# A post-norm attention and feed-forward layer on one core: the instruction lists of all five engines in a new order

## The chip, the cores and the metric

One core of a Trainium2 chip runs one launch of the kernel. The metric is the device time of that launch in microseconds; the median of 3 runs of the kernel before is 277.16 us (276.86 to 277.42). The core has TensorE (PE in the profile), VectorE (DVE), ScalarE (ACT), GpSimd (POOL) and SyncE (SP), whose queue here issues the DMA transfers of the main part.

## The reference

The input `x` is 8 x 1024 x 128 in fp32. One attention head of width 128 and a feed-forward part with a hidden width of 512, each followed by a residual sum and a layer norm, are applied to each of the 8 batches:

```python
q = fractional_rope(einsum('btd,hdk->bhtk', x, wq)) * dh ** -0.5
k = fractional_rope(einsum('btd,hdk->bhtk', x, wk)) * dh ** -0.5
v = einsum('btd,hdk->bhtk', x, wv)
s = einsum('bhik,bhjk->bhij', q, k) - 1e30 * mask      # causal: j > i is masked
o = einsum('bhij,bhjv->bihv', softmax(s), v)
x = layernorm(x + o @ wo)
bw1 = mean(|w1|, axis=1) * sign(w1); bw2 = mean(|w2|, axis=1) * sign(w2)
h = gelu(x @ bw1.T + b1, approximate=False)
x = layernorm(x + h @ bw2.T + b2)
```

The rotation turns the first half of the width only; the second half is left as it is. `wv` and `wo` are multiplied into one matrix `wvo` in the kernel's setup.

## The kernel before

Each of the 8 batches goes through the same chain of steps, and each step is a small Python function of one engine, called with a row or half number and the batch `c`. Every engine's program is a list of such calls, written out by hand in one block per engine; the engines meet through semaphores. Batches overlap: while batch c is in its feed-forward part, batch c+1 is in its scores and batch c+2 in its projections. B is 8, so `B - 1` is batch 7, `B - 4` batch 4 and so on.

The steps of one batch, in order of their data:
- SP loads `xq` (`stripes`, L222) and `xa` (`tokens`, L228). VectorE turns `xq` into `xT` with stream transposes (`x_squares`, L1579). ScalarE rounds it (`xT_high`, L1029) and GpSimd takes the rest (`xT_low`), so that fp32 products are made of three passes (high by high, low by high, high by low).
- TensorE: `project(half, c)` (L654), 12 matmuls into a pair of PSUM banks. VectorE multiplies with cosine and sine (`rotate`, L1597), GpSimd adds (`rotation_sum`), ScalarE copies what isn't rotated into `tok` (`tok_copy`, L1036).
- TensorE: `turn_qk(n, c)` (L668), four transposes into one bank. ScalarE `qkT_high` (L1052), VectorE `qkT_low` (L1617).
- TensorE: `scores(r, c)` (L578), three passes per row block r of 128 queries, up to 1024 columns. VectorE `row_max` (L1451), ScalarE `exponentials` (L994) with the row sum, VectorE `turn_row` (L1460), 32 x 32 transposes, whose blocks SP carries to `probT` by DMA (`carry`, L233). In batches 0 and 7, rows 4 to 7 are transposed by TensorE (`turn_row`) and copied by VectorE and ScalarE (`row_copy`).
- TensorE: `weigh_group(half, ...)` (L593), or `weigh_row(r, c)` (L612) where TensorE turned the rows; ScalarE `pxT_copy` (L1045); TensorE `project_out` (L625); VectorE `residual1` (L1478), `statistics1`, GpSimd `first_factors`, VectorE `first_norm` (L1494).
- TensorE `turn_x1` (L635), ScalarE `x1T_high` (L1058), VectorE `x1T_low` (L1558); TensorE `up(f, c)` (L642), ScalarE `gelu` (L1064) and `hidden_high` (L1071), GpSimd `hidden_low`; TensorE `down` (L678), ScalarE `y_half` (L1089), TensorE `turn_y` (L714), VectorE `residual2`, `statistics2`, GpSimd `second_factors`, ScalarE `second_norm` (L1096), SP `store` (L245).
- The last batch does its feed-forward part in halves: `up_half` (L694), `gelu_half` (L1077), `hidden_high_half` (L1083, on VectorE L1514), `hidden_low_half` (VectorE, L1520), `down_quarter` (L704).

PSUM holds three pairs of banks and two single banks, and TensorE takes them in turn in the order of its calls. Whoever takes a pair waits first until what was put there three pair tasks before has been read: for a projection that is `tok_copy`, for scores the `exponentials`, for `up` the `gelu` (`wait_freed`, L495):

```python
def next_pair(*task):
    pair_of[task] = pairs[len(pair_of) % len(pairs)]
    if len(pair_of) > len(pairs):
        wait_freed(*list(pair_of)[-1 - len(pairs)])
    return pair_of[task]
```

So the order of TensorE's calls sets also which reader a call waits for. `fill(n)` (L557) issues n bf16 matmuls of 512 columns on constants into a free pair; nobody reads their results. ScalarE's exponential and GELU need different tables, so each change between `exponentials` and `gelu` loads a table.

Calls of TensorE's list that the prediction speaks of, with their lines: `fill(2)` L735, `project(1, 3)` L790, `scores(6, 2)` L788, `turn_qk(3, 3)` L805, `turn_x1(1, 1)` L816, `turn_qk(3, B - 3)` L862, `turn_x1(1, B - 2)` L947, `project_out(0, B - 1)` L949, `turn_x1(0, B - 1)` L962, `project_out(1, B - 1)` L963, `up_half(0, 0, B - 1)` L964, `fill(7)` L969, `fill(2)` L972. Of ScalarE's: `xT_high(0, 1)` L1125, `tok_copy(1, 3)` L1180, `gelu(0, B - 2)` L1377, `y_half(0, B - 3)` L1378, `second_norm(0, 3)`. Of VectorE's: `rotate(1, 0)` L1629, `x_squares(0, 1)` L1630, `rotate(1, 3)` L1730.

Of the kernel before, what the change touches and what calls it, by code (L numbers as in the profile page):

```python
# [16 lines left out]
def attention_ffn_kernel(nc, x, wq, wk, wv, wo, w1, b1, w2, b2, cos_t, sin_t, out):  # L17
# [10 lines left out]
    B, T, D = x.shape  # L28
# [27 lines left out]
    with ctx:  # L56
# [147 lines left out]
        def _(sp):  # L204
# [53 lines left out]
            stripes(2)  # L258
            carry(0, 0)
            stripes(3)  # L260
            tokens(1)
# [6 lines left out]
            carry(1, 2)  # L268
            stripes(B - 2)
            tokens(3)  # L270
            carry(0, 3)
            carry(1, 3)
            stripes(B - 1)
            carry(0, B - 4)
            tokens(B - 4)
            tokens(B - 3)
            carry(1, B - 4)
            carry(0, B - 3)
            tokens(B - 2)
            store(0)  # L280
            carry(1, B - 3)
            carry(0, B - 2)
            store(1)
            carry(1, B - 2)
            store(2)
            tokens(B - 1)
            carry(0, B - 1)
# [10 lines left out]
        def _(pool):  # L298
# [99 lines left out]
            xT_low(0, 2)  # L398
            xT_low(1, 2)
            rotation_sum(0, 2)  # L400
            xT_low(0, 3)
            xT_low(1, 3)
            first_factors(0, 0)
            rotation_sum(1, 2)
            rotation_sum(0, 3)
            first_factors(1, 0)
            xT_low(0, B - 4)
            xT_low(1, B - 4)
            rotation_sum(1, 3)
            first_factors(0, 1)  # L410
            first_factors(1, 1)
            rotation_sum(0, B - 4)
            rotation_sum(1, B - 4)
# [3 lines left out]
            xT_low(0, B - 3)  # L417
            hidden_low(3, 0)
            first_factors(0, 2)
            xT_low(1, B - 3)  # L420
            first_factors(1, 2)
            rotation_sum(0, B - 3)
            xT_low(0, B - 2)
# [6 lines left out]
            rotation_sum(1, B - 3)  # L430
            first_factors(1, 3)
            xT_low(1, B - 2)
            hidden_low(0, 2)
            rotation_sum(0, B - 2)
# [4 lines left out]
            xT_low(0, B - 1)  # L439
            first_factors(0, B - 4)  # L440
            second_factors(1)
            first_factors(1, B - 4)
            xT_low(1, B - 1)
            rotation_sum(0, B - 1)
# [4 lines left out]
            second_factors(2)  # L449
            first_factors(0, B - 3)  # L450
            rotation_sum(1, B - 1)
# [33 lines left out]
        def _(pe):  # L485
# [257 lines left out]
            setup_turn_sgn1()  # L743
# [6 lines left out]
            turn_row(4, 0)  # L750
            turn_row(5, 0)
            turn_qk(1, 1)
# [7 lines left out]
            scores(2, 1)  # L760
            weigh_group(0, 0, 3, 0)
            scores(3, 1)
            scores(4, 1)
            scores(5, 1)
            project_out(0, 0)
            scores(6, 1)
            turn_qk(0, 2)
            scores(7, 1)
            weigh_row(4, 0)
            project(1, 2)  # L770
            weigh_row(5, 0)
            weigh_row(6, 0)
            weigh_row(7, 0)
            turn_qk(1, 2)
# [15 lines left out]
            project(1, 3)  # L790
            weigh_group(1, 0, 3, 1)
            turn_x1(1, 0)
            weigh_group(1, 4, 7, 1)
            up(0, 0)
            up(1, 0)
            project_out(1, 1)
            turn_qk(0, 3)
            up(2, 0)
            project(0, B - 4)
            turn_qk(1, 3)  # L800
            turn_qk(2, 3)
            up(3, 0)
            scores(0, 3)
            scores(1, 3)
            turn_qk(3, 3)  # L805
            weigh_group(0, 0, 3, 2)
            scores(2, 3)
            turn_x1(0, 1)
# [5 lines left out]
            scores(6, 3)  # L814
            weigh_group(1, 0, 3, 2)
            turn_x1(1, 1)  # L816
# [5 lines left out]
            up(1, 1)  # L822
            project_out(1, 2)
            turn_qk(2, B - 4)
            project(0, B - 3)
            up(2, 1)
            down(0, 0)
            scores(0, B - 4)
            down(1, 0)
            scores(1, B - 4)  # L830
            up(3, 1)
# [3 lines left out]
            turn_y(1, 0)  # L835
            weigh_group(0, 0, 3, 3)
# [4 lines left out]
            weigh_group(1, 0, 3, 3)  # L841
            scores(5, B - 4)
            scores(6, B - 4)
            weigh_group(1, 4, 7, 3)
# [16 lines left out]
            scores(0, B - 3)  # L861
            turn_qk(3, B - 3)  # L862
            scores(1, B - 3)
# [10 lines left out]
            weigh_group(1, 0, 3, B - 4)  # L874
            project(1, B - 2)
            weigh_group(1, 4, 7, B - 4)
            turn_qk(0, B - 2)
            up(0, 3)
            turn_qk(1, B - 2)
            up(1, 3)  # L880
            project_out(1, B - 4)
            up(2, 3)
            down(0, 2)
            up(3, 3)
            turn_qk(2, B - 2)
            turn_qk(3, B - 2)
            project(0, B - 1)
            down(1, 2)
            turn_y(0, 2)
            scores(0, B - 2)  # L890
            scores(1, B - 2)
            scores(2, B - 2)
            turn_y(1, 2)
            weigh_group(0, 0, 3, B - 3)
            scores(3, B - 2)
            turn_x1(0, B - 4)
            scores(4, B - 2)
# [5 lines left out]
            weigh_group(1, 0, 3, B - 3)  # L903
            turn_qk(0, B - 1)
            weigh_group(1, 4, 7, B - 3)
            up(0, B - 4)
            up(1, B - 4)
            turn_qk(1, B - 1)
            project(1, B - 1)
# [4 lines left out]
            up(2, B - 4)  # L914
            up(3, B - 4)
            scores(0, B - 1)
            turn_y(1, 3)
            weigh_group(0, 0, 3, B - 2)
            scores(1, B - 1)
            turn_qk(2, B - 1)  # L920
            scores(2, B - 1)
            turn_qk(3, B - 1)
            scores(3, B - 1)
            project_out(0, B - 2)
            scores(4, B - 1)
            weigh_group(1, 0, 3, B - 2)
            scores(5, B - 1)
            weigh_group(1, 4, 7, B - 2)
# [1202 lines left out]
```

## Time and profile before

| | us |
|---|---|
| median of 3 runs | 277.16 (276.86 to 277.42) |
| span of the profiled execution | 274.5 |
| PE busy (matmuls) | 260.9, 95% |
| DVE busy | 229.6, 84% |
| ACT busy | 224.7, 82% |
| POOL busy | 167.2, 61% |

The span is that of one execution under the profiler; a run's time has 2.7 us more around it. Matmuls overlap in the array, so that the start of one and the start of the next tell more than the busy time: in a timeline each row gives the start in us, the duration, the engine, the line, the operation with output and inputs, the shape, the count, and in brackets the idle time before it and what ended it.

### The profile page before, as it was taken

What the parts mean: (1) busy time and instruction counts of PE and PEld (TensorE: products, weight loads), DVE (VectorE), ACT (ScalarE), POOL (GpSimd) and SP (SyncE); (2) the same over time, 40 slices, a digit from 0 to 9 for tenths busy, and PEclk for the clock granted to TensorE, in tenths of its full rate; (3) what the DMA queues carried; (4) which work ended last, traced back from release to release, by engine and by line L of the source; (5) the groups of instructions that cost most, each with busy time, mean ns of one, the idle gap of its engine ahead of it and who ended that gap; (6) DMA issues with size and microseconds to landing.
All of it is one profiled execution on the core that took longest, in us unless ns stands there. A gap on an engine that the chain in (4) does not pass through costs nothing.

```text
span 274.5 us, 5184 instructions
## 1 busy us (share of the span) xinstructions
PE 260.9 (95%) x1485; PEld 208.7 (76%) x1487; DVE 229.6 (84%) x638; ACT 224.7 (82%) x398; POOL 167.2 (61%) x258
## 2 busy tenths in 40 slices
PE   7899999999999999999999999999999999999960
PEld 3678989987779588868879688868886878897630
DVE  2799999999999996999979987998689738537984
ACT  3378964565897989996998999898999799999972
POOL 3033132613625698399821998497819887887772
PEclk9999999999999999999999999999999999999997
DMA  7944596479657936833685318825830720200323
GB/s 178 166 61 87 107 145 98 115 163 192 104 132 160 199 94 153 180 47 78 173 187 127 82 39 249 184 71 151 189 73 27 197 55 2 76 2 0 111 90 108
DMA packets 58012, 31.94 MB, mean 116 GB/s; under 512 B 33408, under 2 KB 54400, under 8 KB 57984
## 3 DMA queue, kind: packets, MB, share of 16 engines
q1 hardware_dynamic: 57024, 30.76, 50.4%
q10 hardware_dynamic: 960, 0.85, 1.3%
q8 instruction: 12, 0.20, 0.3%
q14 instruction: 16, 0.13, 0.2%
HBM read 9.18 MB, written 4.19 MB: 49 GB/s over the span
## 4 chain that ended last, share of the span: by engine, by line
PE 81%; DVE 6%; ACT 5%; issue 3%; DMA 2%; ACTq 1%; POOL 0%; POOLq 0%
PE pair L589 18%; PE bank L606 18%; PE bank L632 5%; PE bank L674 4%; PE pair L650 4%; PE pair L651 4%; PE bank L620 4%; PE bank L682 4%; PE bank L683 4%; PE bank L719 2%; DMA sin_sb<-in_sin_dram 2%; PE pair L663 2%; PE pair L665 2%; PE pair L664 2%; PE bank L639 2%
## 5 line engine op out<-in xcount | busy, mean ns | idle before, releaser
L391 POOL TENSOR_TENSOR hid_lo<-hid,hid_hi 128x1024 fp32r<-128x1024 f32 x28 | 66.0, 2386 | 19.7 <-ACT hid_hi L1075 19.7
L1004 ACT ACTIVATE prob<-pair,negmax 128x128 f32<-128x128 f32 (+3 forms) x64 | 47.2, 742 | 14.2 <-DVE negmax L1457 12.5
L606 PE MATMUL bank<-probT,xa 128*128 128x512 f32 (+3 forms) x160 | 54.2, 482 | 0.0
L1457 DVE CUSTOM_DVE_ANT_0 pair<-pair,mask_row 128x128 f32<-128x128 f32 (+3 forms) x64 | 47.9, 759 | 6.1 <-PE pair L589 5.5
L606 PEld LDWEIGHTS bank<-probT,xa 128*128 128x128 f32 x160 | 29.1, 190 | 20.2 <-issue 15.3
L341 POOL TENSOR_TENSOR xT_lo<-xT,xT_hi 128x512 fp32r<-128x512 f32 x14 | 18.0, 1288 | 40.4 <-ACT xT_hi L1034 40.4
L1467 DVE STREAM_TRANSPOSE turned<-prob 128x128 f32<-128x128 f32 (+7 forms) x56 | 39.5, 724 | 0.5 <-ACT prob L1004 0.5
L589 PE MATMUL pair<-qkT_hi 128*128 128x512 f32 (+3 forms) x96 | 36.0, 375 | 0.8 <-DVE qkT_lo L1619 0.3
L1068 ACT ACTIVATE hid<-pair,b_sb,alpha 128x1024 f32<-128x1024 f32 x28 | 32.9, 1209 | 0.1
L589 PE MATMUL pair<-qkT_lo,qkT_hi 128*128 128x512 f32 (+3 forms) x96 | 32.8, 342 | 0.0
L589 PE MATMUL pair<-qkT_hi,qkT_lo 128*128 128x512 f32 (+3 forms) x96 | 32.8, 342 | 0.0
L1075 ACT ACTIVATE hid_hi<-hid 128x1024 fp32r<-128x1024 f32 x28 | 28.6, 1057 | 0.0
L335 POOL TENSOR_TENSOR ln<-ln,minus_half 128x4 f32<-128x4 f32 (+1 forms) x21 | 26.2, 1249 | 1.6
L1102 ACT ACTIVATE res<-res,ln 128x128 f32<-128x128 f32 x52 | 23.1, 496 | 3.6 <-POOL ln L377 3.6
L1056 ACT ACTIVATE qkT_hi<-bank 128x512 fp32r<-128x512 f32 x32 | 18.5, 598 | 7.3 <-PE bank L674 7.2
L1619 DVE TENSOR_TENSOR qkT_lo<-bank,qkT_hi 128x512 fp32r<-128x512 f32 x32 | 21.1, 680 | 3.4 <-ACT qkT_hi L1056 3.4
L349 POOL TENSOR_TENSOR tok<-rot_cos,rot_sin 128x512 f32<-128x512 f32 x14 | 18.0, 1288 | 9.4 <-DVE rot_sin L1614 9.4
L650 PE MATMUL pair<-x1T_hi,sgn1T 128*128 128x512 f32 x56 | 23.4, 418 | 0.3 <-issue 0.3
L682 PE MATMUL bank<-hid_hi,sgn2T 128*128 128x512 f32 x56 | 22.3, 399 | 0.0
L683 PE MATMUL bank<-hid_lo,sgn2T 128*128 128x512 f32 x56 | 22.2, 396 | 0.0
L651 PE MATMUL pair<-x1T_lo,sgn1T 128*128 128x512 f32 x56 | 22.1, 395 | 0.0
L1567 DVE TENSOR_TENSOR res<-bank,x 128x512 f32<-128x512 f32 x16 | 10.9, 687 | 12.5 <-PE bank L719 12.4
(116 smaller groups left out, 649.9 us busy)
## 6 DMA issues: line engine op xcount, KB each, us to landing
probT<-turned SPq DMA_DIRECT2D x96, 116.0 KB, 2.3
probT<-turned SPq DMA_DIRECT2D x128, 52.0 KB, 2.0
xq<-in_L_attn_x_dram SPq DMA_DIRECT2D x28, 128.0 KB, 4.0
xa<-in_L_attn_x_dram SPq DMA_DIRECT2D x7, 512.0 KB, 4.7
out_dram<-res SPq DMA_DIRECT2D x7, 512.0 KB, 3.3
hid<-in_L_ffn_w_dram SPq DMA_DIRECT2D x2, 256.0 KB, 3.2
out_dram<-res SPq DMA_DIRECT2D x2, 256.0 KB, 2.3
xa<-in_L_attn_x_dram SPq DMA_DIRECT2D x1, 256.0 KB, 3.6
```

Source lines behind the costliest of these rows:

```text
L391: pool.tensor_tensor(hid_lo[:, j, :], hid[:, j, :], hid_hi[:, j, :].bitcast(F32), ALU.subtract).then_inc(s_hid_lo[j], 1)
L589: ins = pe.matmul(dst[:, lo:hi], qp[:, 0, me], kp[:, 1, lo - first:hi - first], start=n == 0, stop=n == 2)
L606: ins = pe.matmul(bank_of["px", g, c][:, 0:n * P], xa[c % 2][:, j, :], probT[g][:, :, TG * j:TG * j + n, :].rearrange("p n m i -> p m n i" ...
L650: pe.matmul(dst[:, half(h)], sgn1T[:, j, :], x1T_hi[:, half(h)], start=True, stop=False)
L651: ins = pe.matmul(dst[:, half(h)], sgn1T[:, j, :], x1T_lo[:, half(h)], start=False, stop=True)
L682: pe.matmul(dst[:, :], sgn2T[:, j, :], hid_hi[:, j, half(h)], start=j == 0, stop=False)
L683: ins = pe.matmul(dst[:, :], sgn2T[:, j, :], hid_lo[:, j, half(h)], start=False, stop=j == NF - 1)
L1004: act.activation(prob[r % 3][:, 0:(r + 1) * P], pair_of["score", r, c][:, slice(*columns(r))], ACT.Exp, scale=-1.0, bias=negmax[:, r:r + 1 ...
L1068: act.activation(hid[:, j, :], pair_of["up", j, c][:, :], ACT.Gelu, bias=b1_sb[:, j:j + 1], scale=alpha1[:, j:j + 1]).then_inc(s_gelu[j], 1)
L1075: act.activation(hid_hi[:, j, :], hid[:, j, :], ACT.Copy).then_inc(s_hid_hi[j], 1)
L1457: dve.tensor_tensor_reduce(mine, mine, mask_row[:, T - (r + 1) * P:T], -1.0, -MASKED, ALU.add, ALU.min, negmax[:, r:r + 1]).then_inc(s_max ...
L1467: dve.transpose(turned[g][:, :, squares(r, 0, r), :].rearrange("p k m j -> p m k j"), prob[r % 3][:, 0:(r + 1) * P].rearrange("p (m k j) - ...
```

## The change

The calls of the five engines' lists, and of SP's queue, are put in a new order. No call is added or taken away, no function is changed, and every semaphore and buffer is the same; only which buffer of the rings a call takes follows from the new order. Parts of the diff, cut to what the prediction speaks of; there are some hundred such moves in it.

SP's queue:

```diff
             stripes(2)
+            tokens(1)
             carry(0, 0)
             stripes(3)
-            tokens(1)
...
+            tokens(3)
             stripes(B - 2)
-            tokens(3)
...
+            store(1)
             carry(0, B - 2)
-            store(1)
```

TensorE (head, batches 1 to 3, batch 5, the last two batches):

```diff
+            setup_wvo()
+            scores(2, 0)
+            turn_qk(2, 0)
+            turn_qk(3, 0)
             fill(2)
-            turn_qk(2, 0)
-            scores(2, 0)
             scores(3, 0)
-            setup_wvo()
+            setup_turn_sgn1()
             project(0, 1)
-            turn_qk(3, 0)
             project(1, 1)
...
+            scores(2, 2)
+            scores(3, 2)
             turn_qk(2, 2)
-            scores(2, 2)
             turn_qk(3, 2)
-            scores(3, 2)
+            project(1, 3)
             project_out(0, 1)
             turn_x1(0, 0)
             scores(4, 2)
             scores(5, 2)
             scores(6, 2)
             scores(7, 2)
-            project(1, 3)
+            turn_x1(1, 0)
             weigh_group(1, 0, 3, 1)
-            turn_x1(1, 0)
...
+            turn_qk(3, 3)
             scores(0, 3)
             scores(1, 3)
-            turn_qk(3, 3)
...
+            turn_x1(1, 1)
             weigh_group(1, 0, 3, 2)
-            turn_x1(1, 1)
...
+            scores(1, B - 3)
             turn_qk(3, B - 3)
-            scores(1, B - 3)
...
+            turn_row(5, B - 1)
             turn_x1(0, B - 2)
-            turn_row(5, B - 1)
+            turn_x1(1, B - 2)
             turn_row(6, B - 1)
-            turn_x1(1, B - 2)
...
-            up(2, B - 2)
             down(0, B - 3)
             down(1, B - 3)
             turn_y(0, B - 3)
+            up(2, B - 2)
             up(3, B - 2)
             turn_y(1, B - 3)
             weigh_row(4, B - 1)
             weigh_row(5, B - 1)
+            turn_x1(0, B - 1)
             weigh_row(6, B - 1)
             weigh_row(7, B - 1)
-            turn_x1(0, B - 1)
+            up_half(0, 0, B - 1)
             project_out(1, B - 1)
-            up_half(0, 0, B - 1)
             up_half(0, 1, B - 1)
             down(0, B - 2)
             down(1, B - 2)
             turn_x1(1, B - 1)
-            fill(7)
             turn_y(0, B - 2)
             turn_y(1, B - 2)
-            fill(2)
...
+            fill(7)
+            fill(2)
```

ScalarE (head, batches 2 and 3, the last three batches):

```diff
+            xT_high(0, 1)
             qkT_high(0, 0)
             qkT_high(1, 0)
             tok_copy(1, 0)
-            xT_high(0, 1)
             setup_signs()
             exponentials(0, 0)
+            qkT_high(2, 0)
             exponentials(1, 0)
             xT_high(1, 1)
+            qkT_high(3, 0)
             exponentials(2, 0)
             exponentials(3, 0)
-            qkT_high(2, 0)
-            qkT_high(3, 0)
...
-            exponentials(1, 2)
+            xT_high(0, B - 4)
             exponentials(2, 2)
             exponentials(3, 2)
             x1T_high(0, 0)
+            tok_copy(1, 3)
             exponentials(4, 2)
             exponentials(5, 2)
+            x1T_high(1, 0)
+            xT_high(1, B - 4)
...
+            x1T_high(1, B - 2)
             row_copy(5, B - 1)
             row_copy(6, B - 1)
-            x1T_high(1, B - 2)
+            hidden_high(3, B - 3)
+            second_norm(0, 3)
...
+            y_half(0, B - 3)
             gelu(0, B - 2)
-            y_half(0, B - 3)
+            y_half(1, B - 3)
             gelu(1, B - 2)
-            y_half(1, B - 3)
-            second_norm(0, B - 4)
...
+            y_half(1, B - 2)
             x1T_high(1, B - 1)
-            y_half(1, B - 2)
```

VectorE (head and batch 2 to 3):

```diff
+            x_squares(0, 1)
             rotate(1, 0)
-            x_squares(0, 1)
...
             row_max(3, 2)
+            turn_row(0, 2)
+            qkT_low(2, 2)
+            reciprocals(1, 1)
+            qkT_low(3, 2)
+            rotate(1, 3)
...
```

## Rows read from the trace of the kernel before

**Rows 1.** Two stages: us, busy PE, PEld, DVE, ACT, POOL, granted clock, DMA share, GB/s.

```profile
24.00:90.00 66.00, 65.61 (x421) 56.08 (x420) 63.69 (x167) 47.50 (x96) 24.49 (x44) 1.00 0.67 133
...
230.00:255.00 25.00, 24.12 (x147) 20.53 (x147) 14.89 (x58) 23.30 (x39) 21.09 (x25) 1.00 0.10 31
```

**Rows 2.** Timeline of PE in the tail: two matmuls that follow each other at once.

```profile
257.97 0.39 PE L701 MATMUL pair<-x1T_lo,sgn1T 128*128 128x512 f32 x1
258.20 0.39 PE L700 MATMUL pair<-x1T_hi,sgn1T 128*128 128x512 f32 x1
```

**Rows 3.** The head: tile `xq` (loads, time issued), and timelines of DVE and PE.

```profile
L214 SPq DMA_DIRECT2D xq<-in_L_attn_x_dram x4: 443/1484/3146, 1.8 to 6.1; - x4
...
10.87 0.68 DVE L1611 TENSOR_TENSOR rot_cos<-pair,cos_sb 128x512 f32<-128x512 f32 x1
...
12.13 0.70 DVE L1584 STREAM_TRANSPOSE xT<-xq 128x512 f32<-128x512 f32 x1
...
23.31 0.47 PE L589 MATMUL pair<-qkT_hi 128*128 128x512 f32 x1 [0.26 <-ACT tok L1041]
```

**Rows 4.** Timeline of PE around three gaps of the middle.

```profile
79.53 0.40 PE L651 MATMUL pair<-x1T_lo,sgn1T 128*128 128x512 f32 x1
80.22 0.30 PE L589 MATMUL pair<-qkT_hi 128*128 128x128 f32 x1 [0.28 <-issue]
...
90.59 0.33 PE L589 MATMUL pair<-qkT_hi,qkT_lo 128*128 128x384 f32 x1
90.95 1.12 PE L606 MATMUL bank<-probT,xa 128*128 128x512 f32 x2
...
140.45 0.27 PE L589 MATMUL pair<-qkT_hi,qkT_lo 128*128 128x128 f32 x1
140.88 0.63 PE L674 MATMUL bank<-ident,tok 128*128 128x128 f32 x4 [0.15 <-DVE res L1567]
```

**Rows 5.** Timelines of PE and ACT at the last two batches.

```profile
230.78 1.13 PE L632 MATMUL bank<-wvo,pxT 128*128 128x128 f32 x8 [0.20 <-DVE x1T_lo L1560]
...
232.20 0.47 PE L650 MATMUL pair<-x1T_hi,sgn1T 128*128 128x512 f32 x1 [0.29 <-issue]
...
246.65 0.60 ACT L1049 ACTIVATE pxT<-bank 128x512 f32<-128x512 f32 x1 [0.47 <-PE bank L620]
...
247.39 1.13 PE L632 MATMUL bank<-wvo,pxT 128*128 128x128 f32 x8 [0.34 <-ACT pxT L1049]
248.52 0.50 PE L700 MATMUL pair<-x1T_hi,sgn1T 128*128 128x512 f32 x1
```

**Rows 6.** Timelines of PE and ACT in the tail.

```profile
254.89 1.46 PE L561 MATMUL pair<-warm 128*128 128x512 bf16 x6
...
257.30 0.59 PE L561 MATMUL pair<-warm 128*128 128x512 bf16 x2
...
266.44 0.63 PE L719 MATMUL bank<-ident,yT 128*128 128x128 f32 x4 [0.96 <-ACT yT L1093]
...
254.50 0.60 ACT L1086 ACTIVATE hid_hi<-pair 128x512 fp32r<-128x512 f32 x1 [0.52 <-PE bank L683]
...
258.86 2.09 ACT L1080 ACTIVATE pair<-pair,b_sb,alpha 128x512 f32<-128x512 f32 x3
```

**Rows 7.** Timelines of PE, DVE and ACT around scores(6,2) and project(1,3).

```profile
62.22 0.40 PE L589 MATMUL pair<-qkT_hi 128*128 128x512 f32 x1
...
67.03 0.69 DVE L1611 TENSOR_TENSOR rot_cos<-pair,cos_sb 128x512 f32<-128x512 f32 x1
...
67.20 1.01 ACT L1004 ACTIVATE prob<-pair,negmax 128x896 f32<-128x896 f32 x1 [2.57 <-DVE negmax L1457]
...
68.41 0.60 ACT L1041 ACTIVATE tok<-pair 128x512 f32<-128x512 f32 x1
```

**Rows 8.** Granted clock by stretch, columns as in Rows 1.

```profile
266.00:268.00 2.00, 0.63 (x4) 0.42 (x4) 1.67 (x9) 0.30 (x1) 1.01 (x1) 1.00 0.67 207
...
270.00:271.00 1.00, 0.00 (x0) 0.00 (x0) 0.17 (x1) 0.18 (x1) 0.71 (x2) 0.90 0.08 25
```

More of the change, by code:

```diff
@@ L874, in _ @@
             weigh_group(1, 0, 3, B - 4)
+            weigh_group(1, 4, 7, B - 4)
+            up(0, 3)
+            turn_qk(0, B - 2)
+            turn_qk(1, B - 2)
             project(1, B - 2)
[L876 to L879, printed above, removed]
             up(1, 3)
             project_out(1, B - 4)
+            down(0, 2)
             up(2, 3)
-            down(0, 2)
-            up(3, 3)
             turn_qk(2, B - 2)
@@ L1276, in _ @@
             second_norm(6, 0)
+            hidden_high(1, 2)
+            x1T_high(1, 3)
+            hidden_high(2, 2)
+            hidden_high(3, 2)
+            exponentials(5, B - 3)
+            exponentials(6, B - 3)
+            pxT_copy(1, B - 4)
             second_norm(7, 0)
-            pxT_copy(1, B - 4)
+            exponentials(7, B - 3)
             qkT_high(0, B - 2)
-            xT_high(0, B - 1)
             qkT_high(1, B - 2)
-            tok_copy(1, B - 2)
             gelu(0, 3)
             gelu(1, 3)
+            tok_copy(1, B - 2)
             y_half(0, 2)
@@ L1353, in _ @@
             gelu(0, B - 3)
+            gelu(1, B - 3)
             y_half(0, B - 4)
-            gelu(1, B - 3)
+            y_half(1, B - 4)
             hidden_high(0, B - 3)
-            y_half(1, B - 4)
-            second_norm(0, 3)
+            hidden_high(1, B - 3)
             gelu(2, B - 3)
             gelu(3, B - 3)
-            hidden_high(1, B - 3)
             pxT_copy(0, B - 1)
@@ L1385, in _ @@
             gelu(3, B - 2)
+            second_norm(0, B - 4)
+            x1T_high(0, B - 1)
             hidden_high(2, B - 2)
@@ L1973, in _ @@
-            rotate(1, B - 1)
             residual2(0, 3)
+            statistics1(3, B - 3)
+            statistics2(0, 3)
+            residual2(1, 3)
             row_max(0, B - 1)
+            row_max(1, B - 1)
             first_norm(0, B - 3)
             first_norm(1, B - 3)
-            residual2(1, 3)
+            qkT_low(2, B - 1)
             first_norm(2, B - 3)
             first_norm(3, B - 3)
+            statistics1(4, B - 3)
+            statistics1(5, B - 3)
+            row_max(2, B - 1)
@@ L1981, in _ @@
+            qkT_low(3, B - 1)
+            statistics1(6, B - 3)
+            statistics1(7, B - 3)
+            statistics2(1, 3)
+            residual1(0, B - 2)
+            residual1(1, B - 2)
+            residual1(2, B - 2)
+            row_max(3, B - 1)
+            row_max(4, B - 1)
+            turn_row(0, B - 1)
+            turn_row(1, B - 1)
+            turn_row(2, B - 1)
+            row_max(5, B - 1)
+            turn_row(3, B - 1)
             first_norm(4, B - 3)
+            reciprocals(1, B - 2)
```

599 lines of the change are left out of this document (281 added, 318 removed).

## Prediction, before any run of the change

> **What bounds the kernel now.** I read the table by stage first [rows 1]. TensorE's matmul time fills 65.61 of 66.00 us from 24 to 90 and 24.12 of 25.00 from 230 to 255. VectorE and ScalarE are busy too (63.69 and 47.50 of 66.00 in the first of these stages), but they run behind TensorE and wait for it as often as it waits for them. Busy time of matmuls overlaps, so it doesn't tell how much is free. For that I went through TensorE's timeline by starts: a three-pass matmul of 512 columns can follow the one before after 0.23 us (257.97 to 258.20 in [rows 2]), one of 384 columns after about 0.18 and one of 128 columns after about 0.1. Whatever lies between two starts beyond that is time in which TensorE had nothing to do. Over the whole profile this comes to about 10.4 us:
> - some 3.1 us in the head, before the score products of batch 0 run without a break (the last wait is 0.26 us at 23.31, [rows 3]);
> - 0.7 us from 24 to 33;
> - in the middle 0.45 us at 80.22, 0.2 us at 90.95 and 0.32 us at 140.88 [rows 4], and crumbs of under 0.15 us;
> - late 0.37 us at 230.78, 0.46 us at 232.20, 0.51 us at 247.39 and 0.16 us at 248.52 [rows 5];
> - the rest from 254.9 to the last transpose, the largest the 1.1 us before 266.44 [rows 6].
> No instruction is added or removed by this change, so what it can win is some part of the gaps. Of the 10.4 us about 3 to 4 are within its reach; the head's waits for the first transfers and the tail's chain through GELU are not. What it can lose has no such ceiling.
>
> **Head, +0.4 us (-0.3 to +0.9).** On VectorE x_squares(0,1), the stream transposes of batch 1, moves in front of rotate(1,0). The rotation now starts at 10.87 and the transpose at 12.13 [rows 3]. The transpose needs the last of the four `xq` loads that SP issued from 1.8 to 6.1 us; it had landed by 12.13, when the transpose ran without a wait. Put at 10.95 it waits between 0 and 12.13 - 10.95 = 1.2 us, and takes 0.70 us itself. Then come rotate(1,0), POOL's sum, tok_copy(1,0), turn_qk(1,0) and scores(1,0), all of which TensorE waits for in the head, so up to 0.70 + 1.2 = 1.9 us of this delay is in its path. Against that, a transpose that is early makes project(0,1) early, and setup_wvo, turn_qk(2,0) and turn_qk(3,0) are put ahead of fill(2) and scores(3,0), where TensorE now waits. I take half of the transpose's 0.70 us, 0.35, and a little for the wait: +0.4. The lower end is one closed wait of the size of the one at 23.31; the upper end is 1.2 us of wait less that.
>
> **Middle, -1.0 us (-1.2 to +0.3).** Three gaps have a reason that the reorder takes away. At 80.22 scores(0,3) starts 0.69 us after the last start of up(3,0) (79.53, whose own share is 0.23): 0.45 us. turn_qk(3,3) and VectorE's work for it are now in front. At 90.95 weigh_group(1,...,2) waits for turned probabilities; turn_x1(1,1) is now ahead of it and fills the 0.2 us. At 140.88 turn_qk(3,5) waits for its bank, and scores(1,5) is now ahead of it: 0.32 us. Together 0.97 [rows 4].
>
> The large move is project(1,3), from behind scores(7,2) to before project_out(0,1). It costs nothing by itself: 12 matmuls of 1.44 us in either place. But the pair of buffers it takes comes round again three tasks later, so scores(6,2) now waits for tok_copy(1,3), which waits for rotate(1,3) and row maxima on VectorE. TensorE started scores(6,2) at 62.22 [rows 7]; with project(1,3) ahead it gets there at 62.22 + 1.44 = 63.66. The projection is then done at about 58.9 + 1.44 = 60.3. On VectorE rotate(1,3) stands right behind qkT_low(3,2), and takes 67.03 to 68.38 less 67.03 = 1.3 us, so it ends at about 61.7. On ScalarE tok_copy(1,3) stands behind x1T_high(0,0), which needs turn_x1(0,0), at about 61.9 + 0.6; the copy itself takes 0.60 [rows 7]: it ends at about 63.1. So it is ready some 0.5 us before TensorE asks. What this costs is VectorE's: row_max(4..7,2) come 1.4 to 3.7 us later, and ScalarE already waits for them (2.57 us before 67.20, [rows 7]). I book no stall here; rival D is its failing.
>
> **Late, -1.5 us (-1.9 to 0).** At the end of batch 7, weigh_row(4..7), turn_x1(0,7) and project_out(1,7) stood in this order, and project_out(1,7) waits for pxT_copy right behind the last weigh_row: 0.51 us at 247.39 and 0.16 us behind it. Now turn_x1(0,7) goes between the weigh_rows and up_half(0,0) before project_out(1,7), 4 x 0.23 us of independent matmuls. That covers both: 0.67. At 230.78 and 232.20, 0.37 + 0.46 = 0.83 us are lost behind turn_x1(1,6) and row transposes; the new order has turn_x1(0,6) and turn_x1(1,6) around turn_row(5) and ScalarE takes both x1T_high before the row copies and second_norm(0,3) after them, so the wait for x1T_low at 230.78 closes. Sum 0.67 + 0.83 = 1.5 [rows 5]. Also down(0,5) and down(1,5) go ahead of up(2,6) and y_half(0,5) ahead of gelu(0,6), which only moves a wait that is not there.
>
> **The fills, 0.** fill(7) and fill(2) are 9 matmuls without use, at 254.89 to 257.5 [rows 6], that keep TensorE active. They now stand behind its last transposes, where they take 9 x 0.21 = 1.9 us (1.46 us for six, less the overlap at the end) from about 267.1: until 269, before the last stores. So they cost nothing there, and removing them where they stood wins nothing: from hidden_high_half(0,0) at 254.50 to the last GELU at 258.86 + 2.09 and on to 265 ScalarE has no break, and sets the pace of the tail [rows 6]. That ScalarE instruction waited 0.52 us for TensorE's down(1,6), so the end is 274.5 - 254.5 = 20.0 us after TensorE finishes down(1,6), whatever TensorE does in between.
>
> **Other queues and small stalls, +0.5 us (0 to +1.5).** SP's loads of tokens and stores trade places with carries; each load lands several us before its use, so 0. ScalarE's order changes in some 60 places with the same 13 switches between exponential and GELU: several hand-overs from ScalarE to TensorE are close, and where a switch falls one entry earlier a gap of the size of those found, 0.2 to 0.5 us, opens. I allow for two small ones.
>
> **Sum.** 0.4 - 1.0 - 1.5 + 0 + 0.5 = -1.6 us. Against the profiled execution, 274.5 us of span, that is 272.9; the median of the runs is 277.16, 2.7 more, and keeps that distance: 277.16 - 1.6 = 275.5.
>
> **Rivals.** B, all gaps close and no new ones open, with the head unharmed: following TensorE's new order with each call's own time gave 0.65 us won at 112, 1.0 at 150, 1.6 at 225 and 3.2 at 250: 277.16 - 3.2 = 274.0. For it: nothing in the list of TensorE's calls that waits is visibly nearer to its producer. Against: ScalarE and VectorE are at 80 to 90% in these stages and were followed with their old durations.
>
> C, no net change, 277.1: the late gain isn't kept, because ScalarE's own chain of hidden_high, second_norm and gelu_half from 240 to 265 sets the end and not TensorE's arrival. For it: ScalarE is busy 23.30 of 25.00 us from 230 to 255 [rows 1]. Against: at 246.65 ScalarE had waited 0.47 us for TensorE's input to pxT_copy, which TensorE then waits for at 247.39 [rows 5]: ScalarE was ahead.
>
> D, slower, by one mechanism: VectorE falls behind in batch 2, and TensorE pays at scores(6,2) for tok_copy(1,3). The price is ScalarE's wait there for a row maximum, 2.57 us [rows 7], passed on to TensorE: -1.6 + 2.6 = +1.0, 278.2; and with the three middle gaps not closed, 279.2. It decides when tok_copy(1,3) ends over 0.5 us later than I have it. For it: VectorE is busy 63.69 of 66.00 us there [rows 1], so a delay isn't made up. Against: the same row maxima were late before without TensorE noticing.
>
> E, slower, by the clock: the fills are gone from 254.9 to 257.5, where TensorE now has under 1 us of extra idle. The granted clock was 1.00 from 266 to 268 though TensorE had four transposes in it, and read 0.90 only in the slice 270 to 271, in which TensorE had been idle for a longer stretch than that [rows 8]; so a gap of 1 us should not lower it. If it did fall from 2.4 to 1.2 GHz, 24 matmuls of the last half batch at 0.23 us, 5.6 us, would take twice as long, of which I put some 4 us on the path: -1.6 + 4 = +2.4, 279.6. The Trainium skill (page "TensorE: Matmul & The Clock Gate", section "HAM oscillation — how this bites in real kernels") says that idle stretches between bursts of matmuls send the array back to the half clock, so that each burst starts cold. By that rule the fills are worth keeping and the time would be E's; [rows 8] bear it out only for a longer pause than the one made here, hence its small chance.
>
> **How the numbers follow.** The forecast 275.5 gets 0.50, B 0.12, C 0.12, D 0.20, E 0.06. About 0.2% (0.55 us) is what a measurement can tell from no change. The range goes from a little below B, 273.6, to a little above D's first price, 278.5; left out are D with all gaps kept, E, and the odd case better than B, together about 0.2. Faster by over 0.2%: the forecast and B, 0.62. Within: C, 0.12. Slower: D and E, 0.26.
>
> **What would show it.** TensorE's idle before 80.22, 230.78, 232.20 and 247.39 should be gone; scores(6,2) at about 63.6 should show no wait for `tok`; the transpose before rotate(1,0) should wait for `xq` under 1 us; the granted clock should read 1.00 from 255 to 267, with TensorE's last transpose about 1.6 us earlier. I am wrong if one long wait for VectorE appears between 55 and 100, if the lead of TensorE is there at 250 but the end isn't earlier (C), or if the clock falls between 255 and 260 (E).

## The result, and the profile after

The changed kernel takes 309.59 us (median of 4 runs, 308.76 to 310.49) beside 277.01 us (275.94 to 277.42) of the kernel before: a ratio of 1.1184, interval 1.1138 to 1.1231. It is 32.6 us slower where a gain of 1.6 us was forecast, and far outside the range. The profiled execution has a span of 307.0 us beside 274.5.

The page of after: busy times, and in 40 equal slices the busy share of TensorE and its granted clock.

```profile
PE 270.1 (88%) x1487; PEld 213.2 (69%) x1487; DVE 260.5 (85%) x638; ACT 224.5 (73%) x398; POOL 167.0 (54%) x258
...
PE   8899999979995999979999999299995994969772
...
PEclk9999999999995999999999999779999897999998
```

The work is the same, and ACT's and POOL's busy times are those of before (224.7 and 167.2). VectorE's isn't: 260.5 us for the same 638 instructions that took 229.6. So some VectorE instruction has become longer. The groups by line and form name it; the first row is before's, the second after's, "x64 | busy, mean ns of one".

```profile
L1499 DVE TENSOR_SCALAR x<-res,ln 128x128 f32<-128x128 f32 x64 | 18.7, 340 | 0.6 <-POOL ln L369 0.3
...
L1499 DVE TENSOR_SCALAR x<-res,ln 128x128 f32<-128x128 f32 x64 | 51.8, 855 | 1.2 <-POOL ln L369 1.1
```

Line 1499 is first_norm: x1 = (res1 - mean) * rstd over 128 columns, both tensors in SBUF. Its 33.1 us more account for all of VectorE's 30.9 us, and the other large forms kept their means to within a few per cent. And these instructions are what TensorE waits for (waits of PE: in total, times, longest):

```profile
PE bank L639 <- DVE x L1499: 19.4, 7, 5.8
PE bank L639 <- DVE res L1485: 3.6, 2, 2.1
PE bank L719 <- ACT yT L1093: 1.6, 2, 1.1
PE pair L589 <- ACT prob L1004: 1.5, 1, 1.5
```

The timelines of DVE, POOL and PE around the first long wait show what makes an instruction of 0.34 us last 2.3:

```profile
87.74 0.34 DVE L1499 TENSOR_SCALAR x<-res,ln 128x128 f32<-128x128 f32 x1
...
88.88 4.65 DVE L1499 TENSOR_SCALAR x<-res,ln 128x128 f32<-128x128 f32 x2
...
94.05 1.77 DVE L1499 TENSOR_SCALAR x<-res,ln 128x128 f32<-128x128 f32 x1
...
88.73 7.02 POOL L391 TENSOR_TENSOR hid_lo<-hid,hid_hi 128x1024 fp32r<-128x1024 f32 x3 [0.90 <-ACT hid_hi L1075]
...
91.22 0.34 PE L589 MATMUL pair<-qkT_hi,qkT_lo 128*128 128x384 f32 x1
95.88 1.11 PE L639 MATMUL bank<-ident,x 128*128 128x128 f32 x4 [4.32 <-DVE x L1499]
```

POOL's three hidden_low run back to back from 88.73. The first_norm at 87.74 comes before them and takes 0.34. The two at 88.88 take 4.65 together, one POOL instruction each: taken singly they end at 91.21 and 93.53, and POOL's instructions end at 91.13 and 93.44. The last ends at 95.82, and the third POOL instruction at 95.74. Meanwhile VectorE's x1T_low (PSUM to SBUF) between them takes its usual 0.68 us. TensorE has nothing for 4.3 us. Of the 64 first_norm, 22 take over 0.6 us, and each of the 22 meets a POOL tensor_tensor of 512 or 1024 columns and ends 0.08 to 0.09 us after it; together they are 33 us longer than 0.34 each, 27 of it at hidden_low and 6 at rotation_sum and xT_low. The 42 others show 0.32 to 0.40, as before. Before, all but five of the 64 ran while POOL was between its long instructions, and those five met only the last or the first 0.4 us of one; the longest of the 64, 0.44 us at 225.90, is the one that met the last 0.35 us of a hidden_low. None of the rows ahead of the prediction was about that.

The slow stretches carry a second cost, TensorE's clock. Windows of after, columns as in [rows 1]:

```profile
94.00:96.00 2.00, 0.12 (x1) 0.12 (x2) 2.00 (x3) 0.00 (x0) 2.00 (x2) 0.50 0.00 0
96.00:98.00 2.00, 2.00 (x6) 1.46 (x7) 2.00 (x5) 0.60 (x1) 0.97 (x1) 0.50 0.00 0
98.00:100.00 2.00, 2.00 (x3) 0.67 (x2) 2.00 (x8) 0.00 (x0) 0.00 (x0) 0.50 0.01 4
100.00:102.00 2.00, 2.00 (x5) 0.86 (x4) 2.00 (x7) 0.55 (x2) 0.50 (x1) 0.90 0.90 143
```

During the wait, in which TensorE was idle from 91.56, the clock fell from 2.4 to 1.2 GHz (a granted clock of 0.50 is 1.2 GHz) and stayed there to 100, with the matmuls that followed spaced twice as wide. There are four such stretches, behind TensorE's waits that end at 95.88, 198.31, 236.62 and 256.87. In them TensorE works 4.5, 4.5, 3.4 and 3.4 us at 1.2 GHz, some 16 us, which costs about half of that, 8 us. This is an estimate; with the 24.5 us of waits on the first, second and fourth row above it gives 32.5, nearly all of the 32.6.

The rows of after that answer to those of the prediction: TensorE is busy 64.24 us of 24 to 90 and 19.91 of 230 to 255 [rows 1].

```profile
24.00:90.00 66.00, 64.24 (x414) 55.30 (x414) 63.63 (x162) 47.21 (x96) 25.31 (x45) 1.00 0.62 125
...
230.00:255.00 25.00, 19.91 (x94) 15.34 (x92) 19.45 (x33) 18.05 (x27) 19.66 (x31) 0.93 0.20 55
```

### The profile page after: what moved, and what is told of

It is laid out like the page before. It is cut to its first block, busy times and chain, and to the rows that moved or that the text cites. A ratio compares the mean times of both kernels' runs of the same rounds, so it can differ in the third digit from the quotient of the medians.

```text
span 307.0 us, 5188 instructions
## 1 busy us (share of the span) xinstructions
PE 270.1 (88%) x1487; PEld 213.2 (69%) x1487; DVE 260.5 (85%) x638; ACT 224.5 (73%) x398; POOL 167.0 (54%) x258
## 4 chain that ended last, share of the span: by engine, by line
PE 44%; DVE 33%; issue 8%; POOL 6%; ACT 5%; DMA 2%; ACTq 1%; POOLq 0%; DVEq 0%
DVE x L1499 12%; PE bank L606 11%; PE pair L589 8%; DVE pair L1457 4%; DVE turned L1467 3%; PE pair L650 3%; PE pair L651 3%; PE bank L674 3%; POOL hid_lo L391 3%; PE bank L682 2%; PE bank L683 2%; DMA sin_sb<-in_sin_dram 2%; PE bank L632 2%; PE bank L639 2%; ACT res L1102 2%
## 5 line engine op out<-in xcount | busy, mean ns | idle before, releaser
L606 PE MATMUL bank<-probT,xa 128*128 128x512 f32 (+3 forms) x160 | 56.9, 506 | 0.0
L1499 DVE TENSOR_SCALAR x<-res,ln 128x128 f32<-128x128 f32 x64 | 51.8, 855 | 1.2 <-POOL ln L369 1.1
L606 PEld LDWEIGHTS bank<-probT,xa 128*128 128x128 f32 x160 | 31.2, 200 | 25.7 <-issue 20.8
L1467 DVE STREAM_TRANSPOSE turned<-prob 128x128 f32<-128x128 f32 (+7 forms) x56 | 38.7, 715 | 0.8 <-ACT prob L1004 0.8
L639 PE MATMUL bank<-ident,x 128*128 128x128 f32 x64 | 11.7, 312 | 23.3 <-DVE x L1499 19.4
L323 POOL TENSOR_TENSOR ln<-stat 128x4 f32<-128x4 f32 (+1 forms) x21 | 4.4, 208 | 40.7 <-DVE stat L1490 38.3
L639 PEld LDWEIGHTS bank<-ident,x 128*128 128x128 f32 x64 | 8.0, 156 | 26.6 <-DVE x L1499 21.9
L1102 ACT ACTIVATE res<-res,ln 128x128 f32<-128x128 f32 x52 | 21.9, 485 | 3.8 <-POOL ln L377 3.6
```

The source lines that it names most:

```text
L606: ins = pe.matmul(bank_of["px", g, c][:, 0:n * P], xa[c % 2][:, j, :], probT[g][:, :, TG * j:TG * j + n, :].rearrange("p n m i -> p m n i" ...
L1102: ins = act.activation(res2[c % 2][:, t, :], res2[c % 2][:, t, :], ACT.Identity, bias=ln2[:, 6, t:t + 1], scale=ln2[:, 7, t:t + 1])
L1467: dve.transpose(turned[g][:, :, squares(r, 0, r), :].rearrange("p k m j -> p m k j"), prob[r % 3][:, 0:(r + 1) * P].rearrange("p (m k j) - ...
L1499: ins = dve.tensor_scalar(x1[c % 2][:, t, :], res1[:, t, :], ln1[:, 2, t:t + 1], ln1[:, 7, t:t + 1], ALU.subtract, ALU.mult)
```

## The experiments

My theory: VectorE's first_norm can't run while POOL is in a long instruction on SBUF, since both want the same port, and whichever began first holds it for its whole length. The runs here can show that the two exclude each other; that a port is the reason is the skill's. The Trainium skill states this mechanism (page "SBUF — State Buffer", section "Who interferes with whom"): VectorE's second pair of SBUF ports is GpSimd's, the pair is an exclusive lock, and a tensor_scalar from SBUF to SBUF is among the operations that can take it, though not in the form that also writes out its accumulator. The rows above agree with the first part; the second part gives an experiment. Rivals: the order itself makes VectorE late; POOL as an engine is overloaded by its new list; SP's queue; the ring of pairs; the missing fills.

**e1: the changed order, first_norm off the shared port.** One edit, and a small tile `unused` for it:

```diff
-                                        ALU.subtract, ALU.mult)
+                                        ALU.subtract, ALU.mult, accum_out=unused[:, t:t + 1])
```

> The changed order, with one edit: first_norm's tensor_scalar also writes a sum of its row into an unused column, so that VectorE takes the instruction at one element per cycle through its own port (the output it computes is the same, the extra column is read by nobody). Port theory: in the changed kernel 26 of the 64 first_norm instructions take 0.8 to 2.4 us instead of 0.34 because each lies inside a POOL instruction; with this form none should, so VectorE's 33 us of stretch go and the time falls from 309.6 to between 276 and 284 (the form itself costs some 0.1 to 0.2 us x 64 on VectorE). Rival, order alone (later batches' work arrives late whatever port is used): the instructions wait where they did, time stays over 300.

Measured: 280.02 us, ratio 1.0104 (1.0070 to 1.0138). By-form rows of e1:

```profile
L1500 DVE TENSOR_SCALAR_CACHE_REDUCE x<-res,ln 128x128 f32<-128x128 f32 x64 | 22.7, 398 | 1.2 <-POOL ln L370 1.1
...
L1500 DVE DVE_READ_ACCUMULATOR x<-res,ln 128x1 f32 x64 | 5.4, 84 | 0.0
```

The longest of the 64 is 0.41 us. An edit that makes every first_norm slower by itself (398 + 84 ns for 340) makes the kernel 29.6 us faster. (The 26 long ones in the expectation were a miscount; the rows give 22. In e3's, 28 and 5 us should be 27 and 6.) The rival falls for all but the last 3 us.

**e2: the old order with the same edit.**

> The old order with the same edit of first_norm, as the control. Port theory: no first_norm was stretched before, so nothing is won; the longer form costs VectorE 6 to 13 us of busy time, mostly hidden: 277 to 281. The difference between e1 and this run is what the order is worth without the port: by my prediction's sum -1.6 us.

Measured: 276.67 us, ratio 1.0008 (0.9990 to 1.0027). Nothing was stretched before, and the longer form hides wholly.

**e3: the changed order, POOL held back.** In POOL's hidden_low, ahead of its own wait:

```diff
+                while unscaled:
+                    h, c = unscaled.pop()
+                    pool.wait_ge(s_x1[h], c + 1)
```

where first_factors adds (h, c) to the list.

> The changed order, with POOL held back: before each hidden_low POOL waits until the first_norm group whose factors it has already made is done. Nothing is left out. Port theory: the stretches that lie inside hidden_low (28 of the 33 us) go, those inside rotation_sum and xT_low (5 us) stay: 280 to 288. Rival, order alone: POOL gets later, so the time gets worse than 309.6.

Measured: 290.92 us, ratio 1.0521 (1.0473 to 1.0570), above the expected band. Ten first_norm are still over 0.6 us, 10.0 us longer in sum than 0.34 each: eight at rotation_sum and xT_low, and two of batch 7, whose factors are made by another function, so that they weren't gated (3.7 us of the 10.0; TensorE waits 3.05 us at 256.70 for them). That POOL, made later, makes the kernel 18.7 us faster speaks against every theory in which POOL or its list is too slow. It isn't free: TensorE now waits 1.0 to 1.6 us three times for hid_lo from 226 to 246.

**e4: the changed order with POOL's old list.**

> The changed order on SP, TensorE, ScalarE and VectorE, POOL's list as before. Port theory: what counts is when POOL's long instructions run against first_norm, and POOL's list moved few of the hidden_low calls, so most of the collisions stay: 300 to 312, with the stretch of first_norm over 20 us. Rival: the new POOL list is what is wrong (xT_low and rotation_sum ahead of hidden_low), then 277 to 285.

Measured: 318.41 us (one run), above both expectations. 16 first_norm are long, by 24.5 us in sum, fewer than in the change, but TensorE also waits 4.2 us at 104.81 and 2.7 at 225.04 for xT_low and rotation_sum, which the old list has behind hidden_low. So POOL's new list isn't what is wrong, as far as one run tells: the other lists need it, and the collisions come with either.

**e6: the long POOL instruction in halves.** 1024 columns of hidden_low become two instructions of 512:

```diff
-                pool.tensor_tensor(hid_lo[:, j, :], hid[:, j, :], hid_hi[:, j, :].bitcast(F32),
-                                   ALU.subtract).then_inc(s_hid_lo[j], 1)
+                for h in range(NG):
+                    ins = pool.tensor_tensor(hid_lo[:, j, half(h)], hid[:, j, half(h)],
+                                             hid_hi[:, j, half(h)].bitcast(F32), ALU.subtract)
+                ins.then_inc(s_hid_lo[j], 1)
```

> The changed order with hidden_low, POOL's longest instruction (2.4 us), issued as two instructions of 512 columns (1.3 us each). Nothing is left out. Port theory, with a first_norm held for the rest of the POOL instruction that it meets: each stretch inside hidden_low should be 1.2 us at most in place of 2.3, so that of 28 us some 14 go: 292 to 300. Rival: if POOL as a whole holds VectorE up (its list being too long), two instructions in place of one cost the same or more: 309 or above.

Measured: 295.84 us (one run), within the band. Timelines of DVE and POOL of e6 at the place shown above:

```profile
89.33 2.51 DVE L1501 TENSOR_SCALAR x<-res,ln 128x128 f32<-128x128 f32 x2
...
92.36 0.71 DVE L1501 TENSOR_SCALAR x<-res,ln 128x128 f32<-128x128 f32 x1
...
89.20 5.01 POOL L392 TENSOR_TENSOR hid_lo<-hid,hid_hi 128x512 fp32r<-128x512 f32 x4 [1.13 <-ACT hid_hi L1077]
```

Two first_norm take 2.51 in place of 4.65: each one is held for one POOL instruction, whatever its length. With half the length the sum of the stretches falls from 33.0 to 22.8 us, though more of the 64 meet an instruction (27 for 22), and the time falls by 13.8 us. This separates a lock that lasts for an instruction from a general slowdown, which would not care how POOL's work is cut.

**e5: what is left of e1: SP's queue.** e1 is still 3.4 us above e2. Its TensorE has one long wait, for the transfers of carry(1,6), and the clock falls behind it. Timelines of PE and SP, and windows, of e1:

```profile
209.47 4.97 PE L607 MATMUL bank<-probT,xa 128*128 128x512 f32 x7 [2.27 <-DMA probT<-turned]
...
182.80 0.39 SPq L250 DMA_DIRECT2D out_dram<-res  x1
183.40 11.12 SPq L243 DMA_DIRECT2D probT<-turned  x16
194.56 1.22 SPq L232 DMA_DIRECT2D xa<-in_L_attn_x_dram  x2
195.88 10.63 SPq L243 DMA_DIRECT2D probT<-turned  x16
...
210.00:212.00 2.00, 2.00 (x3) 0.67 (x2) 1.44 (x7) 2.00 (x6) 2.00 (x2) 0.50 0.00 0
```

A carry is 16 issues of about 0.63 us, 10 us of SP's time, and carry(0,6) and carry(1,6) stand nearly in a row. In the kernel before the first of them starts at 178.39 and the second has landed at 201.93. In e1 store(1) is ahead of the first, which starts at 183.40, and tokens(6) and tokens(7) are ahead of the second, which lands at 209.43. e5 is e1 with SP's old list.

> As e1 (the changed order, first_norm in the form that keeps to VectorE's own port), but SP's queue in its old order. In e1 TensorE waits 2.27 us at 209.47 for the transfers of carry(1,6), and the granted clock falls to 0.50 behind it. In e1's queue store(1) stands before carry(0,6) and holds it from 178 to 183, and tokens(6), tokens(7) stand before carry(1,6). Queue theory: with the old queue the wait and the slow clock behind it go, some 2.3 + 1.8 = 4.1 us: 276 (275.3 to 277). Rival: the wait comes from VectorE's turn_row of batch 6, which is late in the new order whatever SP does: 279 to 280.

Measured: 277.63 us, ratio 1.0020 (0.9993 to 1.0046), between the two expectations: above the queue theory's 277 and under its rival's 279. Its profile has neither the wait nor a slice of slow clock: the second carry lands at 206.91, and the matmul group starts at 207.44. So SP's new list costs 2.4 us here, less than the 4.1 expected, and the part of the theory on store(1) is wrong. VectorE's transposes of row 3 of batch 6, first in e1, then in e5, and SP of e5:

```profile
182.66 0.71 DVE L1468 STREAM_TRANSPOSE turned<-prob 128x512 f32<-128x512 f32 x1
...
183.05 0.71 DVE L1468 STREAM_TRANSPOSE turned<-prob 128x512 f32<-128x512 f32 x1
...
183.79 10.02 SPq L243 DMA_DIRECT2D probT<-turned  x16
193.86 0.58 SPq L250 DMA_DIRECT2D out_dram<-res  x1
194.54 10.58 SPq L243 DMA_DIRECT2D probT<-turned  x16
```

In both runs carry(0,6) starts 0.03 us after these transposes end, at 183.40 and 183.79, with or without the store ahead of it. The 5 us that it is later than before come from VectorE, as the rival said: in e5 the exponentials of row 3 end at 178.5, but VectorE's new list has four first_norm and a row maximum ahead of its transposes. This leaves TensorE 0.5 us of room in e5. SP's new list takes that room by what comes behind: from the first carry's first issue to the second's it takes 12.48 us in e1 and 10.75 in e5, and the last transfer lands 3.5 us after its issue in place of 2.4. Which of the moved entries does this (the store before the first carry, or the two loads before the second) wasn't told apart.

**e7: the head alone.** Old order, with the change's first part on TensorE, ScalarE and VectorE.

> The old order with the change's head alone (TensorE's, ScalarE's and VectorE's lists up to the row transposes of batch 0; POOL and SP as before). By my sum +0.4 us (-0.3 to +0.9), so 276.8 beside a before of 276.4; the rival says that the early transposes win what the closed waits are worth: -0.3.

Measured: 276.84 us, ratio 0.9998 (0.9969 to 1.0026): no difference, with an interval too wide to tell the forecast's +0.4 from the rival's -0.3. The step's own uncertain cost is there to read in e7's timeline of DVE, within its bounds of 0 and 1.2 us, and in after it was 0:

```profile
11.73 0.71 DVE L1584 STREAM_TRANSPOSE xT<-xq 128x512 f32<-128x512 f32 x1 [0.70 <-DMA xq<-in_L_attn_x_dram]
```

**e8 and e9: the end alone, on either port.** Old order with the change's last part on the three engines, the fills moved; e9 is e8 with e1's edit.

> The old order with the change's end alone: TensorE from up(2,6) on, ScalarE from gelu(0,6) on, VectorE from first_norm(0,7) on, the fills behind TensorE's last transposes. By my sum the gaps at 247.39 and 248.52 close and the fills' going costs nothing: -0.67 us, 275.7. Rival C: the end is ScalarE's and the gain isn't kept: 276.4. Rival E: TensorE's clock falls without the fills: 278 to 280.

> e8 (the old order with the change's end alone, 281.0 us) with first_norm in the form that keeps to VectorE's own port. In e8 the four first_norm of batch 7's first half take 4.8 us in place of 1.1, inside two hidden_low, and TensorE waits 3.05 us for them; one more first_norm, in a part that e8 leaves as it was, is held 2.3 us at 125.03. Port theory: both go, and the time with them: 275.5 to 277. Rival, VectorE's new order at the end (residual2 of batch 5, which waits 2.57 us for a store, ahead of first_norm of batch 7): the wait of TensorE stays, 279 to 281.

Measured: e8 281.01 us, ratio 1.0132 (1.0085 to 1.0178); e9 276.50 us, ratio 0.9982 (0.9956 to 1.0007). So a reorder of the last tenth of the lists goes with 4.5 us of collisions, and costs nothing that can be told without them. e8's timelines of DVE, POOL and PE, batch 7:

```profile
243.14 4.80 DVE L1499 TENSOR_SCALAR x<-res,ln 128x128 f32<-128x128 f32 x4
...
242.68 4.67 POOL L391 TENSOR_TENSOR hid_lo<-hid,hid_hi 128x1024 fp32r<-128x1024 f32 x2 [0.76 <-ACT hid_hi L1075]
...
248.00 1.12 PE L639 MATMUL bank<-ident,x 128*128 128x128 f32 x4 [3.05 <-DVE x L1499]
```

Two of the four first_norm paid, the other two then passed when POOL was done. And e8 holds a second case, in a part of the lists that it leaves as they were. First before, then e8, VectorE and POOL at 125 us:

```profile
125.03 0.34 DVE L1499 TENSOR_SCALAR x<-res,ln 128x128 f32<-128x128 f32 x1
...
122.84 4.77 POOL L391 TENSOR_TENSOR hid_lo<-hid,hid_hi 128x1024 fp32r<-128x1024 f32 x2
...
125.03 2.62 DVE L1499 TENSOR_SCALAR x<-res,ln 128x128 f32<-128x128 f32 x1
...
122.85 4.72 POOL L391 TENSOR_TENSOR hid_lo<-hid,hid_hi 128x1024 fp32r<-128x1024 f32 x2
```

Both issue first_norm at 125.03, and the POOL pair starts 0.01 us apart. Before slips in at the seam between the two (0.34), e8 doesn't, is held for the whole second one, and TensorE loses 1.7 us at 129.92. That is part of the 4.5 us and isn't the reorder's. What decides it isn't in these rows: in before, in e8 and in e7 first_norm starts 0.20 us ahead of the end of a POOL instruction with another right behind, and it slips in twice (before; e7, 0.34 at 125.64) and is held once. The old order has this coin toss in it too, and where first_norm is on its own port it is gone. It may be why e8's six runs spread from 278.4 to 281.8 us, of which the profiled one is the longest; no other profile shows that.

**e10: the fills back.** e5 with fill(7) and fill(2) between the transposes again.

> e5 (the changed order, first_norm on its own port, SP's queue as before, 277.6 us) with fill(7) and fill(2) back between the transposes where they stood. My prediction put the fills at nothing: 277.6, no change, since ScalarE sets the pace of the tail. Rival E: they keep the clock or the tail's start up: e5's tail takes 20.3 us from the last down product to the end, before's 20.0, so 0.3 us at most, and more only if the clock falls: 277.3.

Measured: 277.80 us, ratio 1.0030 (1.0001 to 1.0060), against e5's 1.0020 (0.9993 to 1.0046). No difference that can be told.

**e11: the late gaps alone.** e2 with two moves; on TensorE:

```diff
             weigh_row(5, B - 1)
+            turn_x1(0, B - 1)
             weigh_row(6, B - 1)
             weigh_row(7, B - 1)
-            turn_x1(0, B - 1)
-            project_out(1, B - 1)
             up_half(0, 0, B - 1)
+            project_out(1, B - 1)
```

and x1T_high(0,7) ahead of hidden_high(2,6) on ScalarE.

> The old order with first_norm on its own port (e2, 276.67 us) and only two moves of the change: on TensorE turn_x1(0,7) between the weigh_rows and up_half(0,0) ahead of project_out(1,7), on ScalarE x1T_high(0,7) ahead of hidden_high(2,6). By my sum the gaps at 247.39 and 248.52 close: -0.67 us, 276.0, and TensorE's last down product of batch 6 ends 0.67 us earlier. Rival C: TensorE is earlier but the end isn't: 276.7.

Measured: 276.77 us, ratio 0.9990 (0.9962 to 1.0019), beside e2's 276.67 and 1.0008. By the times alone 0.67 us could hide in the intervals; the timelines say more. Timelines of PE, first e2, then e11:

```profile
247.75 1.13 PE L633 MATMUL bank<-wvo,pxT 128*128 128x128 f32 x8 [0.34 <-ACT pxT L1050]
...
248.34 1.13 PE L633 MATMUL bank<-wvo,pxT 128*128 128x128 f32 x8
...
254.74 0.66 PE L640 MATMUL bank<-ident,x 128*128 128x128 f32 x4 [0.60 <-DVE x L1500]
```

The gap before project_out(1,7) is closed and the last down product ends 0.6 us earlier (254.14 for 254.73), as forecast. But the matmuls that fill the gap push project_out(1,7) itself 0.59 us back, and from it hangs the chain of the second half of batch 7: residual1, statistics, factors, first_norm, turn_x1(1,7). This comes 0.17 us later than in e2, behind a new wait of 0.60 us. What I had as the start of the fixed tail, down(1,6), was only the later of two.

**e12: what showed no loss, together.** Head of e7 and end of e9, middle, POOL and SP as before, first_norm on its own port.

> The old order with the change's head and end, the middle as before, POOL's list and SP's queue as before, and first_norm on its own port: the parts of the change that showed no loss (e7: 276.84 beside 276.52, e9: 276.50 beside 276.55). If their gaps add up, 276.0, under both kernels by 0.5 us; if the head's gain is spent in the fixed tail, 276.5 and no difference.

Measured: 276.00 us beside 276.39, ratio 0.9971 (0.9943 to 0.9999). It is the fastest here, 33 us under the change and, if the interval is taken at its word, just under the kernel before.

## Why the prediction was wrong, point by point

**The step that failed stands in no single term: it is the premise under all of them.** I went through the new order with "each call's own time" and wrote of rival B that ScalarE and VectorE "were followed with their old durations". For first_norm the duration isn't the instruction's own. It is 0.34 us while POOL is between long instructions, and otherwise what is left of the POOL instruction that it meets plus 0.08 us, up to 2.4 us. The old order kept the two apart; that was a property of the order, and the one that the change gave up. No rival had it: D came nearest (VectorE late, TensorE pays), but with a ready price of 2.6 us at one place, which was wrong in place, size and cause. Its sign, a long wait for VectorE between 55 and 100, did appear (4.32 us before 95.88), from first_norm and not from the row maxima. The range was built from TensorE's gaps, and nothing bounded VectorE's and POOL's times against each other.

What I could have read in the trace of before: 64 tensor_scalar instructions on VectorE, and beside them POOL, whose instructions of 512 and 1024 columns (hidden_low 66.0, xT_low 18.0, rotation_sum 18.0 us by the page of before) fill 37% of the span. By chance alone some 24 of the 64 would overlap one (in after, 23 do); in before five did, at an edge. The one at 225.90 that took 0.44 us was the only sign in a duration that a rule was at work.

**Head, +0.4.** e7: 0 within 0.3%, an interval that holds +0.4 too. The transpose's wait was 0.70 us in e7 and 0 in after, inside the bounds. Whether the rest was hidden stays open.

**Middle, -1.0.** In e5, which shows the order without the collisions, the gap at 80.22 is gone. The other two aren't: TensorE still loses 0.31 us before weigh_group at 91.33 and 0.42 us before turn_qk at 141.67, each 0.1 more than before. So of 0.97 us only some 0.24 came. The working for project(1,3) held: in after scores(6,2) starts at 63.02 and in e5 at 63.72, forecast 63.6, without a wait. Rival D's place was free of loss; the wait in after is one task later, 1.54 us at 65.95 for an exponential that hangs on two held first_norm at 61.64.

**Late, -1.5.** All four gaps close in e5, where TensorE loses some 0.7 us from 230 to 250 beside 1.9 before, counted by starts as in the prediction. Yet e11 shows that the 0.67 us of the last two are no gain, since project_out(1,7) is moved back by nearly as much as is won.

**Fills, 0.** Right: e10 against e5. The tail from the end of the last down product is 20.0 to 20.8 us in before, after, e2, e5, e9, e10 and e11, forecast 20.0. That it was longest in e11, where that product came early for its surroundings, shows that the 20 us weren't a constant but the longer of two chains.

**SP's queue, 0.** Wrong: 2.4 us (e1 against e5). I looked whether the moved loads land before their use, and not at what is queued behind them: in e1 carry(1,6) lands 2.5 us later than in e5, and TensorE waits for it. It also took VectorE's new order, which starts the carry before it 5 us later than in the kernel before and uses up the room.

**Small stalls, +0.5.** Two gaps of 0.4 us that weren't there before stand in e5, before turn_qk at 29.55 and before weigh_group at 54.73, so the allowance was about right. With port and queue set right, the order is worth nothing that can be told: e5's 1.0020 against e2's 1.0008, with intervals that overlap.

**Rival E.** The place was wrong, the mechanism was in play: the clock fell in or behind TensorE's waits of 4.3, 5.8 and 3.9 us and two of 1.5 and 1.6 us in a row, and in e1 behind one of 2.3. By the rule that the prediction cites from the Trainium skill, pauses in the matmul stream send the array back to half speed, and these rows bear it out. But it doesn't follow from the pause alone: in after TensorE waited 3.05 us before 276.36 with a granted clock of 1.00 from 274 to 280, and in e8 3.05 us before 248.00 with 0.50 from 248 to 250.

So of the 32.6 us 29.6 go with first_norm's form (e1), 2.4 more with SP's queue (e5), and the last 0.6 aren't told from nothing. This split hangs on the order in which the causes were taken out: in after TensorE has no wait for a transfer, and the queue costs something only once the collisions are gone. The forecast also put a run's time 2.7 us above the span; a profiled run's time is 1.8 us above its own span (308.76 for 307.0), and nothing hangs on it here.

## What to carry to other kernels

Before a reorder is costed with the durations of the old trace, ask of each instruction whether its duration is its own: lay VectorE's SBUF-to-SBUF tensor_scalar beside GpSimd's long instructions, and where a tuned order shows hardly any overlap, take that as a rule to keep. Where it can't be kept, the form with an accumulator output (0.48 us for 0.34) buys independence, and shorter GpSimd instructions shrink each collision. A gap closed on the busiest engine is won only if what is put in it doesn't push back the head of another chain; and in a queue, price a moved entry by what then stands behind it.

## What was not expected of the hardware

- POOL's power function doesn't hold VectorE up: in after first_norm at 125.61 takes its 0.34 us inside the 1.04 us of the row below, which works on 4 columns. Only the instructions of 512 and 1024 columns did.

```profile
125.17 1.04 POOL L335 TENSOR_TENSOR ln<-ln,minus_half 128x4 f32<-128x4 f32 x1
...
125.61 0.34 DVE L1499 TENSOR_SCALAR x<-res,ln 128x128 f32<-128x128 f32 x1
```

- While POOL's instructions follow each other at once, VectorE gets in only one at a time: each further first_norm is held again, 2.33 and 2.40 us in a row from 88.88.
- The outcome at a seam isn't told by the starts: 0.20 us ahead of it, first_norm took 0.34 us in before and e7 and 2.62 in e8.
- TensorE's clock fell to half just behind a wait of 2.27 us (e1) and neither in nor behind one of 3.05 us (after, 276.36).
